# Scattering rows by expert from GpSimd: the wait for the landing moved from behind each group of four DMAs to ahead of the group's next rewrite

## What is computed

```python
xn = layernorm(x)
# attention: 14 means of 64 keys each, and the last 128 keys as they are
probs = softmax(masked(q_sem @ k_sem2 + rope(q_geo) @ k_geo2) * scale)
attn = (probs @ v2) @ Wo
# experts: the 4 likeliest of 16 for each token
scores = softmax(xn @ router_w.T + expert_bias)
top_w, top_idx = top_k(scores, 4); top_w /= sum(top_w)
ffn = sum_k top_w[k] * (silu(xn @ gate[e_k]) * (xn @ up[e_k])) @ down[e_k]
out = x + attn + ffn
```

## Time and profile before

| | us |
|---|---|
| median of two timed runs | 454.5 |
| the two runs | 455.62 and 453.37 |
| the profiled execution's own time | 455.62 |
| its span, first to last instruction | 453.8 |
| mean granted TensorE clock, share of full speed | 0.909 |

### The profile page before, as it was taken

One profiled execution on the slowest core, in us unless ns is written; L12 is line 12 of the kernel. 1 busy time (PEld: TensorE's weight loads), 2 busy tenths in 40 slices (PEclk: granted clock), 3 DMA queues, 4 the chain that ended last, 5 costly groups with the idle time before them and its releaser, 6 DMA issues.

```text
span 453.8 us, 8919 instructions
## 1 busy us (share of the span) xinstructions
PE 369.9 (82%) x2249; PEld 317.8 (70%) x2250; DVE 253.5 (56%) x832; ACT 190.6 (42%) x648; POOL 244.1 (54%) x211
## 2 busy tenths in 40 slices
PE   0789349697898793688786999999999999998970
PEld 0687246576785573466664999999999999888860
DVE  4885683468524684299942555555554555444530
ACT  1665000566521552144331555555555555444530
POOL 2600266564656337998600466666656666548573
PEclk9998857888999897699865999999999999999995
DMA  8959021121227943735124566676666666556543
GB/s 263 341 171 237 12 83 70 71 84 60 75 85 237 303 133 102 225 101 168 48 69 117 95 110 110 100 122 108 113 101 103 111 98 115 101 93 105 66 53 45
DMA packets 51544, 54.50 MB, mean 120 GB/s; under 512 B 5808, under 2 KB 47680, under 8 KB 51520
## 3 DMA queue, kind: packets, MB, share of 16 engines
q1 hardware_dynamic: 36880, 34.87, 26.6%
q0 software_dynamic: 14640, 19.34, 25.6%
HBM read 30.92 MB, written 23.27 MB: 119 GB/s over the span
## 4 chain that ended last, share of the span: by engine, by line
PE 36%; DMA 24%; POOL 14%; issue 12%; DVE 8%; POOLq 3%; SPq 2%; ACT 1%; DVEq 0%
PE bank L1200 30%; POOL xn_by_expert L637 11%; DMA xn_by_expert<-x_all,slot_i 11%; DMA out_rows<-y,idx 10%; PE bank L1529 3%; PE bank L1547 2%; POOL out_rows L659 2%; POOLq L652 1%; DMA x_all<-in_L_attn_x 1%; DMA xcT<-xn_turned 1%; POOL x_all L634 1%; DVE q L1025 1%; DVE q L1022 1%; SPq L497 1%; DVE pr L1125 1%
## 5 line engine op out<-in xcount | busy, mean ns | idle before, releaser
L659 POOL DMA_INDIRECT out_rows<-y,idx x79 | 122.0, 1545 | 103.1 <-ACT y L823 67.2
L637 POOL DMA_INDIRECT xn_by_expert<-x_all,slot_i x64 | 65.4, 1023 | 20.2 <-issue 15.7
L1200 PE MATMUL bank<-wgu_hi,xh 128*128 x158 | 65.4, 414 | 5.6 <-issue 3.2
L1184 DVE SCALAR_TENSOR_TENSOR act<-bank,xg,sg 128x224 f32<-128x224 f32 x79 | 35.6, 450 | 56.2 <-ACT sg L810 51.8
L1200 PE MATMUL bank<-wgu_lo,xh 128*128 x158 | 58.7, 371 | 0.0
L1200 PE MATMUL bank<-wgu_hi,xl 128*128 x158 | 58.1, 368 | 0.0
L1179 DVE TENSOR_TENSOR xl<-bank,xh 128x256 fp32r<-128x256 f32 x79 | 33.5, 425 | 41.8 <-ACT xh L806 36.0
L810 ACT ACTIVATE sg<-bank 128x224 f32<-128x224 f32 x79 | 28.3, 358 | 59.9 <-PE bank L1200 55.7
L1200 PE MATMUL bank<-wdn_hi,ah 112*128 x158 | 51.3, 324 | 1.0 <-issue 0.5
L823 ACT COPY y<-bank 128x256 f32<-128x256 f32 x79 | 29.5, 374 | 40.7 <-PE bank L1200 18.3
L1200 PE MATMUL bank<-wdn_hi,al 112*128 x158 | 44.4, 281 | 0.0
(11 more groups left out here) (219 smaller groups left out, 795.5 us busy)
## 6 DMA issues: line engine op xcount, KB each, us to landing
xg<-xn_by_expert SPq DMA_DIRECT2D x79, 129.0 KB
wgu<-in_L_ffn_gate_proj SPq DMA_DIRECT2D x16, 224.0 KB, 3.7
wgu<-in_L_ffn_up_proj SPq DMA_DIRECT2D x16, 224.0 KB, 4.2
wdn<-in_L_ffn_down_proj SPq DMA_DIRECT2D x16, 224.0 KB, 4.5
x_all<-in_L_attn_x SPq DMA_DIRECT2D x8, 256.0 KB, 4.6
xr<-in_L_attn_x SPq DMA_DIRECT2D x16, 128.0 KB, 2.1
out_rows<-xr SPq DMA_DIRECT2D x16, 128.0 KB
xn_turned<-xT SPq DMA_DIRECT2D x7, 256.0 KB, 2.6
```

Of the source, the lines that this page charges most:

```text
L637: gp.indirect_dma_start(xs_d, bass.IndirectOffsetOnAxis(slot_i[:, z, r:r + 1], 0), x_all[:, z, :], None).then_inc(xs_in[q], DMA)
L659: gp.indirect_dma_start(out_rows, bass.IndirectOffsetOnAxis(idx[r % RING][:, 0:1], 0), ysb[r % 4][:, :], None, compute_op=ALU.add).then_in ...
L1184: nc.vector.scalar_tensor_tensor(av[t.par][:, :], bank[2 + t.par][:, I:2 * I], xg[t.slot][:, D + 1:D + 2], sg[t.par][:, :], ALU.mult, ALU. ...
L1200: return nc.tensor.matmul(o, lhsT, rhs, start=start, stop=stop)
```

## The change

In the scatter loop the wait for a group's DMAs is taken out from behind the group. For the second, third and fourth expert choice (r of 1 to 3) a wait for the same semaphore is put in front of the copy that rewrites the group's weight column; it asks for the DMAs of the choice before. The wait behind the last group is gone. Nothing else is changed.

```diff
             for r in range(K):
                 gp.wait_ge(weights_ready, r + 1)
                 for q in range(GROUPS):
+                    if r:
+                        gp.wait_ge(xs_in[q], r * GT * DMA)
                     nc.gpsimd.tensor_copy(x_all[:, q * GT:(q + 1) * GT, D + 1], weight[:, r, q * GT:(q + 1) * GT]).then_inc(meta_ready, 1)
                     gp.wait_ge(meta_ready, r * GROUPS + q + 1)
                     for z in range(q * GT, (q + 1) * GT):
                         gp.indirect_dma_start(xs_d, bass.IndirectOffsetOnAxis(slot_i[:, z, r:r + 1], 0), x_all[:, z, :], None).then_inc(xs_in[q], DMA)
-                    gp.wait_ge(xs_in[q], (r + 1) * GT * DMA)
```

## The result

The changed kernel took 500.3 us (median of two runs, 499.4 to 501.3) against 454.5: a ratio of 1.090, interval 1.070 to 1.111. I had forecast 445.0. Its profiled execution has a span of 499.3 against 453.8, 45.5 us more. All eleven executions on record lie between 491.1 and 503.4.

The account below looks back on a forecast made before the run. The scatter's end was taken as the bound, through SP's 8.7 us wait at L563. Terms -8.7 - 1.0 - 0.3 = -10.0, eased to -9.5, took 455.62 to 446.1; 1.1 less for the median gave 445.0, range 440.0 to 450.5.

Parts of the forecast that it names:

- More DMAs in flight: POOL's scatter loop: up to eight or so DMAs in flight instead of four, taken as no cost; upper bound 21 us late.
- the four rivals: Alternative outcomes for the whole kernel: 449 (chance 0.17), 441.0 (0.12), 454.5 (0.05) and 464.7 us (0.04).
- the slower one: Rounds 0 to 2: six experts' splits lock VectorE for their full length, +10.2 us net, 464.7; chance 0.04.
- The rest of the sum: Terms for SP's wait at L563 (-8.7), TensorE's clock (-1.0), moved splits (-0.3) and SP's chain (half a microsecond off).
- the stretching in front: VectorE in rounds 0 to 2, beside POOL's earlier splits: 5.1 us of stretching, +1.7 of it on the path.
- the clock: TensorE at round 3's start: less idle before it, so a less cold start, -1.0 us (between 0 and -2.5).
- rounds 4 and 5: Later rounds, relieved of POOL's splits: 4 us of stretching and waiting show there, half of it, 2.0, should go.
- 169.0 for the weights and 172.5 for the rows: SP behind L563: its wait gone, -8.7 us, so the fourth pair's weights and tile 4's rows are issued at these times.
- forecast was a start between 176 and 179: Sign on TensorE: round 3 starts then instead of at 185.38, after some 2.5 us idle.
- the three that the text costed: VectorE's operations with both inputs in SBUF, L1029, L1132 and L1147, stretched beside POOL's splits: 0.85 us for each expert.
- The expert stage is a block, as said: Behind round 5: nothing changes, the expert stage shifts as a block and is as long as before.
- the second rival: Later rounds run undisturbed, round 3 warm and rounds 4 and 5 at 9.80: -13.5 us, 441.0; chance 0.12.

Follow-up runs that it names:

- e16_changed_fourth: The changed kernel, not altered in anything, run again in the sixth set on the chip of the fifth: 441.5 us, ratio 0.973.
- e5_changed_again: The changed kernel, not altered in anything, run again in the third set: 501.6 us, ratio 1.107.

## Why the prediction was wrong

*The step that failed* is the one under "More DMAs in flight": "The lower bound is no cost", "I take no cost". It bounded what denser issuing does to POOL's own issue time, and that was right: 996 ns and 1028 ns against 1023. It didn't ask what POOL's landing waits did for the others. In the late sets these waits were the gaps in which TensorE's signals got through. Their removal costs 57.2 us in the local stage, while everything behind it is 12.0 shorter. None of the four rivals had this mechanism; the slower one, at 464.7, rested on VectorE being locked by POOL's low splits for six experts. That happens for about three of them (below), and it isn't what makes the late sets slow.

*The trace of before had a row that I didn't follow.* In its own window from 80 to 150 us:

```profile
DVE l L1049 <- remote: 2.8, 2, 1.8
DVE osb L1067 <- remote: 2.2, 1, 2.2
ACT lpT L749 <- remote: 0.9, 1, 0.9
```

In a program of one core, 5.9 us of waits ended by "remote" have no owner. In the prompt trace of the changed kernel there are none. The first trace thus came from a late set, as its count of recorded updates says too, and showed the delay in small, held down by sixteen pauses: TensorE's updates for VectorE's scores are recorded 0.08 to 1.89 us behind the matmul there, against 0.07 or 0.08 in e16_changed_fourth. I had the window open for other reasons and passed over it.

*The rest of the sum* can be checked against e16_changed_fourth, where the signals are prompt, and its mechanism holds, while three of its terms were mis-sized (the stretching in front, the clock, rounds 4 and 5) and one agreement is luck. This sets a prompt trace beside the late one of before, so that part of each difference can belong to the condition:

- POOL: the loop runs from 54.47 to 144.43, forecast 146; the front waits never stop it.
- SP, timeline of e16_changed_fourth, against the earlier trace rows; no wait at L563 is left, and the text had 169.0 for the weights and 172.5 for the rows:

```profile
168.96 0.40 SPq L359 DMA_DIRECT2D wgu<-in_L_ffn_gate_proj  x1
...
172.45 0.90 SPq L527 DMA_DIRECT2D xcT<-xn_turned  x2
```

- TensorE, against the earlier trace rows; forecast was a start between 176 and 179:

```profile
150.30 3.64 PE L1201 MATMUL bank<-wqg,xcT 128*128 128x512 f32 x4 [3.38 <-DMA xcT<-xn_turned]
...
177.06 3.31 PE L1201 MATMUL bank<-wqg,xcT 128*128 128x512 f32 x4 [3.17 <-DMA xcT<-xn_turned]
```

  Here two things met. The local stage was 3.5 us shorter (128.25 against 131.75), which no term had, and rounds 0 to 2 were 2.3 longer: the two groups of matmuls that were at 153.06 and 168.06 are 16.57 apart instead of 15.00, 1.6 for which the text had 1.7, and the stretch before them 22.05 instead of 21.31.

  That SP sends the weights at 168.96, as forecast, is luck. It comes to L563 at 168.46 against 168.51, though the local stage ended 3.5 us sooner: its way through rounds 0 and 1, where it stores VectorE's sum at 164.98 against 164.35, became longer by the same 3.5, and the text had 1.7 for that.
- VectorE's stretching moved, but there was more of it in front than the 5.1 us of the sum: in rounds 3 to 5 L1030, L1133 and L1148 take 973, 855 and 388 ns against 1413, 1172 and 589, in rounds 0 to 2 884, 972 and 1338 against 693, 392 and 388. By these means and counts it is at least 8.6 us in rounds 0 to 2. When POOL's first splits begin, at 145.98, three pieces of VectorE's work grow at once:

```profile
149.28 2.41 DVE L1143 TENSOR_SCALAR ssum<-ssum,const_k 128x32 f32<-128x32 f32 x1
...
152.12 4.50 DVE L1148 TENSOR_TENSOR pr<-pr,srec 128x224 f32<-128x224 f32 x2
```

  Before they took 0.24 and 0.70. L1143 ends at 151.69 and POOL's split instruction beside it at 151.65; the two of L1148 end at 155.24 and 156.61, those beside them at 154.99 and 156.36. So VectorE was held to the end of the GpSimd instruction each time, as the slower rival had it, only not for all six experts. L1143 is a fourth operation that stretches, beside the three that the text costed.
- The clock and the rounds behind: round 3 to the first result scatter takes 62.16 us (177.06 to 239.22) against 67.65 (185.38 to 253.03). That is 5.5 less, where I had put 1.0 for the clock and 2.0 for rounds 4 and 5. The terms were too small; how the 5.5 divides between clock, stretching and condition no run separates.
- From the first projection to the first result scatter it is 110.97 against 121.28, so -10.3 where the sum said -9.5; in the late trace -12.0. The expert stage is a block, as said: from the first result scatter to the end 201.0 and 201.1 us against 200.8.

With prompt signals the time is 441.5, within the range given, but by 3.5 us of the local stage that no term had and by rounds that gave back more than was put down for them. It is near the second rival's 441.0, whose round 3 was to be warm; it took 3.31 for its first four matmuls, nearer to the 3.78 of before than to 1.88; with late ones it is 500.3 to 501.9, and the trace of one set can't tell which of the two a later set will meet.

*What is shown and what isn't.* Shown: in four traces of the changed kernel out of five, in different sets, TensorE's signals are late in the local stage while POOL issues, from some 25 us into the scatter on and not behind its end; within one set, on one chip, the time is 448 us with gaps behind every group and 502 without (fifth set), 472 with four gaps and 501 without (fourth set); pauses in POOL's issuing let them through, whether or not a landing is waited for; and the same program on the same chip has them prompt in another set. In all four late traces VectorE resumes the same time after POOL's last scatter DMA has been issued: 4.5, 4.6, 4.6 and 4.5 us (141.64 to 146.15, 139.03 to 143.65, 141.81 to 146.45, 140.50 to 145.04), whenever its matmuls had ended (117.97, 139.20, 142.72 and 128.73). Not shown: on which path the signals are held, why TensorE's and not ScalarE's, and what makes a set late or prompt. A theory that fits all runs is a path shared by TensorE's signals and by what each scatter DMA sends out on completion, which falls behind a dense stream and catches up in gaps. No experiment separated it from others. One rival is untested: the recording itself. In the late traces fewer updates are recorded, every execution on record comes with a span and a granted clock of its own, and so none is known to have run unrecorded; whether the recording takes part in the delay is open.

The kernel before hardly shows which condition it ran in: its medians are 452.7 and 454.3 in the prompt sets, and 454.5, 452.8, 454.7 and 452.4 in the late ones. The traces say why that can be so. Its round 3 waits for the scatter's end, where SP stands 8.7 us at L563 in one trace and 6.3 in the other, so a local stage that ends sooner only makes SP wait longer. The same shows in one kernel that has traces of both kinds: with the landing waits left out for the first choice alone, the local stage ends at 128.4 in the prompt set and at 133.9 in the late one, SP waits 7.0 and 1.2 us, and the times are 447.7 and 448.1. Whether it is so for the kernel before is not shown, as it has no trace from a prompt set.

## What to carry to other kernels

Before you remove a wait, ask not only who waits for it but what its idle time lets through: in some sets, a stream of indirect DMAs without gaps held up signals of an engine that shares nothing with it in the program. A "remote" releaser in a program of one core was a signal that came late, and was worth following even where it was 2 us. Put the kernel under question, unaltered, in every set of experiments, or a change in the surroundings passes for a cure; and prefer the version that wins in both: a pause of about 1.5 us behind every group, or the group's landing wait from the second choice on, came out 1.0 to 1.7% below the kernel before in either condition, where the changed kernel is 2.7% below it or 9 to 11% above.

## What the runs showed of the hardware that I had not expected

TensorE's signals to ScalarE and VectorE arrived up to 31.6 us behind the matmul in the first trace (84.39 to 115.95) and 53.0 us in e5_changed_again (84.18 to 137.18), at a DMA share of 0.26 and 94 GB/s in the first. The Trainium skill (Advanced Engine Details and Errata, "DMA Bandwidth Details") gives the overhead of a semaphore increment as about one cycle on this chip. That is a cost of DMAs, not a time of delivery, and no run here measures it; the delivery of TensorE's updates took 0.01 to 0.08 us in the prompt trace of the changed kernel, over the local stage, and the times above in the late ones. The Trainium skill's rule that DMA never contends with a compute engine (SBUF — State Buffer, "Who interferes with whom") is about SBUF's ports, and the trace agrees: L1050 takes 298 ns late and 297 prompt. It says nothing of the signals between engines.

POOL's split instructions held VectorE to their own end in e16_changed_fourth: L1143 took 2.41 us instead of 0.24, and the two of L1148 took 4.50 instead of 0.70, each ending 0.04 to 0.25 us behind the split instruction beside it.

The condition is a matter of the set: all traces of a set fall on the same side by their count of recorded updates, and between two sets on one chip the same program took 501.9 and 441.5 us.
